# Byte addresses for the experts' weights, and second layers issued one block later

## The chip, the cores and the metric

The kernel runs on one core of a Trainium2 chip. The metric is the device time in microseconds of one execution, as the median of several runs. Engines are named as in the profile: PE is the matrix engine (PEld its weight loads, PEq and PEldq what its instruction queue does besides), DVE the vector engine, ACT the scalar engine, POOL the general one, SP the one that only starts DMAs.

## What is computed

The input (16 sequences of 113 tokens, 256 wide, 1808 tokens in all) goes through eight layers with residuals. Two of them are layers of experts, and only those are touched:

```python
# layer 0: 15 experts, 3 for each token
h = jnp.einsum('td,efd->etf', xt, fc1_w) + fc1_b[:, None, :]        # 256 -> 512
xh, g = (h[..., :F], h[..., F:])
a = jax.nn.gelu(g, approximate=False) * xh * geglu_mult[:, None, :]  # 256
yexp = jnp.einsum('etf,edf->etd', a, fc2_w) + fc2_b[:, None, :]      # 256 -> 256
y = jnp.einsum('etd,te->td', yexp, comb)
# layer 3: 8 experts, 1 for each token
for e in range(n_experts):
    h = jax.nn.relu(xt @ w1[e] + b1[e])                              # 256 -> 1024
    y = h @ w2[e] + b2[e]                                            # 1024 -> 256
    out = out + ((sel_t == e).astype(xt.dtype) * wgt_t)[:, None] * y
```

## The kernel before

Float32 numbers are carried as two float16 halves, a high and a low one, and a product is three matmuls (`mm3`, L455 to L459): high by high, high by low, low by high. In the profile these are lines L457, L458 and L459, for all products of the kernel, so that the tile names tell which product it is. In this text three such matmuls are called a three.

A stage before the experts (`stage_route`) sorts the tokens by expert into blocks of 128 and gives each block its expert's number, in a small table that is known only when the kernel runs. `stage_experts` then goes over the blocks: 57 in the layer of 15 experts (tiles m0x_...), 23 in the layer of 8 (m3x_...). For each block n:

- POOL gathers the 128 token rows from DRAM with an indirect DMA (`gather`, xg, four buffers) and copies the expert's bias (`bias`, b1, two buffers). In its program gather n+3 stands before bias n, and bias n waits until `lo_ready` says that block n-2 is through.
- PE turns the tokens (`turn`, four transposes, L1511, into pt), ACT copies them into SBUF (`take_tokens`, L1562, xb).
- PE does the first layer (`first`, into ph, two buffers): in m0x 4 x 2 threes of 128 columns, in m3x 8 x 2.
- m0x: ACT makes the gate with Gelu (L1573), DVE the product (L1607, a), ACT its high half (L1578, ah), DVE the low half (L1619, al). m3x: ACT makes the high half with Relu straight from ph (L1582, eight instructions), DVE the same in float32 (L1613, eight), then the low half (L1619).
- PE does the second layer (`second`, into py, two buffers): in m0x 2 threes of 256 columns, in m3x 8.
- DVE scales the result (L1625, yo), SP stores it (L1644).

All weights of all experts lie in SBUF, `w1_hi`, `w1_lo`, `w2_hi` and `w2_lo`. Which one a matmul reads depends on the expert's number, so that PE's instruction stream holds register instructions ahead of matmuls, which compute the address. [...]

The order of the work is written out by hand for PE: turn 0, turn 1, first 0, and then for each n: turn n+2, first n+1, second n. ACT and DVE follow: ACT takes tokens n+2 and does `hidden` n+1 (gate and high half); DVE does `hidden` n+1 (product and low half) and then output n. Other layers' weights are prepared between blocks (`prepare`, m0x alone).

Of the kernel before, what the change touches and what calls it, by code (L numbers as in the profile page):

```python
# [6 lines left out]
F16 = mybir.dt.float16  # L7
# [9 lines left out]
D = 256  # L17
# [1102 lines left out]


# [314 lines left out]
def stage_experts(nc, core, m, prepare=None):  # L1436

    N, NF, FH = m.blocks, m.NF, m.FH  # L1440
    with Stage(nc, m.name + "x") as st:
        two, four = range(2), range(4)
# [6 lines left out]
        a_hi, a_lo = ([st.sb(f"{n}{p}", [128, FH, 128], F16) for p in two] for n in ("ah", "al"))  # L1449
# [8 lines left out]
                "y_out", "stored"))  # L1458
        if prepare is not None:
            prepare = prepare(st)  # L1460
        with nc.Block() as block:  # L1461
            @block.gpsimd
            def _(pool):
                if prepare is not None:
                    prepare.on_pool(pool)

                def gather(at):
                    p, before = at.of(4)

# [24 lines left out]
            @block.tensor  # L1494
            def _(pe):
# [9 lines left out]
                def turn(at):  # L1505
                    (p, before), (q, uses) = at.of(2), at.of(4)
                    pe.wait_ge(gathered[q], uses * 16 + 16)

                    need(pe, xb_ready[p], before)
# [5 lines left out]
                def first(at, e):  # L1515
                    p, before = at.of(2)
                    pe.wait_ge(xb_ready[p], before + 1)
# [10 lines left out]
                def second(at, e):  # L1528
                    p, before = at.of(2)

                    need(pe, y_out[p], before)
                    pe.wait_ge(hi_ready[p], before + 1)
                    pe.wait_ge(lo_ready[p], before + 1)
                    for f in range(FH):
                        w = [w[:, bass.ds(e, 1), f, :].rearrange("p a n -> p (a n)") for w in (m.w2_hi, m.w2_lo)]
                        last = mm3(pe, py[p][:, 0:D], a_hi[p][:, f, :], a_lo[p][:, f, :], w[0], w[1],
                                   f == 0, f == FH - 1)
                    last.then_inc(y_ready[p], 1)

                turn(At(0, 0))  # L1540
                turn(At(0, 1))
                ahead = expert(0)
                first(At(0, 0), ahead)
# [12 lines left out]
            def _(act):  # L1556
                def take_tokens(at):
                    (p, before), (q, uses) = at.of(2), at.of(4)
                    act.wait_ge(turned[q], uses + 1)

                    need(act, h_ready[p], before)
# [3 lines left out]
                def hidden(at):  # L1565
                    p, before = at.of(2)
                    act.wait_ge(h_ready[p], before + 1)
                    act.wait_ge(b1_ready[p], before + 1)
                    if m.gelu:

                        need(act, a_ready[p], before)
                        for f in range(FH):
                            ins = act.activation(gate[p][:, f, :], ph[p][:, FH + f, :], ACT.Gelu,  # L1573
                                                 bias=b1[p][:, 0, FH + f:FH + f + 1], scale=1.0 / WS)
                        ins.then_inc(gate_ready[p], 1)
                        act.wait_ge(a_ready[p], before + 1)
                        need(act, y_ready[p], before)
                        act.activation(a_hi[p][:], act32[p][:], ACT.Copy).then_inc(hi_ready[p], 1)  # L1578
                    else:
                        need(act, y_ready[p], before)  # L1580
                        for f in range(FH):
                            ins = act.activation(a_hi[p][:, f, :], ph[p][:, f, :], ACT.Relu,  # L1582
                                                 bias=b1[p][:, 0, f:f + 1])
                        ins.then_inc(hi_ready[p], 1)

                def step(at):
                    take_tokens(at + 2)
                    hidden(at + 1)

                take_tokens(At(0, 0))  # L1590
                take_tokens(At(0, 1))
                hidden(At(0, 0))
                for n in range(N - 2):
                    step(At(0, n))
                    if prepare is not None:
                        prepare.on_scalar(act, n)
                hidden(At(0, N - 1))

            @block.vector
            def _(dve):  # L1600
                def hidden(at):
                    p, before = at.of(2)
                    if m.gelu:
                        dve.wait_ge(gate_ready[p], before + 1)
                        need(dve, hi_ready[p], before)
                        for f in range(FH):
                            ins = dve.scalar_tensor_tensor(act32[p][:, f, :], ph[p][:, f, :], b1[p][:, 0, f:f + 1],  # L1607
                                                           gate[p][:, f, :], ALU.add, ALU.mult)
                        ins.then_inc(a_ready[p], 1)
                    else:  # L1610
                        dve.wait_ge(hi_ready[p], before + 1)
                        for f in range(FH):
                            ins = dve.tensor_scalar(act32[p][:, f, :], ph[p][:, f, :], b1[p][:, 0, f:f + 1], 0.0,  # L1613
                                                    ALU.add, ALU.max)
                        ins.then_inc(a_ready[p], 1)
                        dve.wait_ge(a_ready[p], before + 1)
                    dve.wait_ge(hi_ready[p], before + 1)
                    need(dve, y_ready[p], before)
                    dve.tensor_tensor(a_lo[p][:], act32[p][:], a_hi[p][:], ALU.subtract).then_inc(lo_ready[p], 1)  # L1619

                def output(at):
                    p, before = at.of(2)
                    dve.wait_ge(y_ready[p], before + 1)
                    need(dve, stored[p], before * 16)
# [3 lines left out]
                def step(at):  # L1628
                    hidden(at + 1)
                    output(at)  # L1630

                hidden(At(0, 0))
                for n in range(N - 1):
                    step(At(0, n))
                    if prepare is not None:
                        prepare.on_vector(dve, n)
                output(At(0, N - 1))
# [1356 lines left out]
```

## Time and profile before

| | us |
|---|---|
| three runs | 1645.15, 1646.43, 1638.35 |
| median | 1645.15 |
| the profiled execution | 1638.66 |
| its span in the profile | 1636.9 |
| m0x stage, first weight matmul to last (57 blocks) | 457.5 to 635 |
| m3x stage, the same (23 blocks) | 1448.7 to 1607.2 |
| PE busy over the span | 1145.5 (70%) |
| DVE | 1097.2 (67%) |
| ACT | 676.8 (41%) |
| POOL | 477.6 (29%) |

The span is what the profiler saw between the first and the last instruction; 1.8 us lie around it. Times in the views are microseconds from the span's start. PE's durations overlap, since matmuls are pipelined: what counts is the distance from one start to the next.

### The profile page before, as it was taken

Reading aid. Unit: us, or ns where it says so; the run is one execution under the profiler, and the core shown is the slowest. Engines: PE = TensorE matmul, PEld = TensorE weight load, DVE = VectorE, ACT = ScalarE, POOL = GpSimd, SP = SyncE. Lnnn points to the kernel's source line nnn. Section 1 sums busy time; section 2 is a strip of 40 time slices with the busy share of each in tenths; the row PEclk is TensorE's granted clock in tenths of the full one; section 3 lists DMA queues with packets and bytes.
Section 4 is the critical chain, followed back from the end, with each engine's and each line's share of the span. In section 5 each row is a group of like instructions: output and inputs, shape, how many; then the busy total and the mean of one; then the engine's idle time right before and its main releaser. Section 6 shows DMA issues by size and latency. Waiting matters only on the chain. (4 is left out here: it accounts for less than half of the span.)

```text
span 1636.9 us, 31503 instructions
## 1 busy us (share of the span) xinstructions
PE 1145.5 (70%) x9868; PEld 802.0 (49%) x9868; DVE 1097.2 (67%) x2322; ACT 676.8 (41%) x1332; POOL 477.6 (29%) x614
## 2 busy tenths in 40 slices
PE   4514877773489998776757866466588885479991
PEld 2211232223367775454446744244467774468881
DVE  4864999984836554657867655787677776445552
ACT  4514655552045443214426522343366554124430
POOL 0042777762344443720001100000133322222103
PEclk9557999995589999886977977687565555579996
DMA  6500000001032333311000000000022221111113
GB/s 213 180 2 10 1 1 0 1 1 46 13 130 86 112 87 128 90 33 78 1 1 1 1 0 0 0 0 0 28 85 95 77 78 52 46 30 44 44 28 107
DMA packets 33969, 78.92 MB, mean 48 GB/s; under 512 B 6840, under 2 KB 22900, under 8 KB 30964
## 3 DMA queue, kind: packets, MB, share of 16 engines
q1 hardware_dynamic: 26800, 57.51, 10.2%
q0 software_dynamic: 6912, 18.88, 4.2%
q8 instruction: 69, 1.13, 0.3%
q10 hardware_dynamic: 144, 1.05, 0.2%
q14 instruction: 44, 0.35, 0.1%
HBM read 61.38 MB, written 16.04 MB: 47 GB/s over the span
## 5 line engine op out<-in xcount | busy, mean ns | idle before, releaser
L942 POOL TENSOR_TENSOR scan_ch<-scan_hs,scan_ct 128x452 f32<-128x452 f32 x128 | 143.5, 1142 | 58.6 <-DVE scan_hs L1054 41.7
L967 PE MATMUL scan_py<-scan_ch,ident 128*128 128x452 f32 x256 | 131.5, 604 | 40.7 <-POOL scan_ch L942 31.0
L1054 DVE TENSOR_TENSOR_SCAN scan_hs<-scan_abar,scan_bx 128x452 f32<-128x452 f32 x128 | 132.8, 1077 | 0.7 <-ACT scan_abar L1016 0.5
L2524 POOL TENSOR_TENSOR mha_prob_lo<-mha_prob,mha_prob_hi 113x452 f16<-113x452 f32 x64 | 65.5, 1044 | 137.8 <-ACT mha_prob_hi L2685 137.8
L457 PE MATMUL m0x_ph<-m0x_xb,m_w_hi 128*128 128x128 f16 x456 | 103.5, 228 | 0.2
L458 PE MATMUL m0x_ph<-m0x_xb,m_w_hi 128*128 128x128 f16 x456 | 100.0, 221 | 0.0
L459 PE MATMUL m0x_ph<-m0x_xb,m_w_lo 128*128 128x128 f16 x456 | 99.8, 220 | 0.0
L1613 DVE TENSOR_SCALAR m3x_a<-m3x_ph,m3x_b 128x128 f32<-128x128 f32 x184 | 49.7, 342 | 73.9 <-ACT m3x_ah L1582 73.9
L967 PEld LDWEIGHTS scan_py<-scan_ch,ident 128*128 128x128 f32 x256 | 41.2, 194 | 111.3 <-POOL scan_ch L942 99.9
L1016 ACT ACTIVATE scan_abar<-ssm_dt,ssm_a 128x448 f32<-128x448 f32 x128 | 80.6, 638 | 23.0 <-DVE scan_hs L1054 21.7
L1046 DVE TENSOR_TENSOR scan_bx<-scan_pb,ssm_dx 128x452 f32<-128x452 f32 x128 | 72.8, 609 | 12.2 <-PE scan_pb L954 12.2
L1607 DVE SCALAR_TENSOR_TENSOR m0x_a<-m0x_ph,m0x_b,m0x_gate 128x128 f32<-128x128 f32 x114 | 34.7, 346 | 65.5 <-ACT m0x_gate L1573 65.1
L1582 ACT ACTIVATE m3x_ah<-m3x_ph,m3x_b 128x128 f16<-128x128 f32 x184 | 50.1, 383 | 65.8 <-PE m3x_ph L459 65.8
L457 PE MATMUL m3x_ph<-m3x_xb,m_w_hi 128*128 128x128 f16 x368 | 76.5, 227 | 0.2
L458 PE MATMUL m3x_ph<-m3x_xb,m_w_hi 128*128 128x128 f16 x368 | 74.9, 223 | 0.0
L459 PE MATMUL m3x_ph<-m3x_xb,m_w_lo 128*128 128x128 f16 x368 | 74.9, 222 | 0.0
L2517 POOL MEMSET mha_v_hi<- 113x768 f16 x1 | 0.7, 738 | 244.3 <-POOLq L638 244.3
L1473 POOL DMA_INDIRECT m0x_xg<-m_rows,m0x_idx x57 | 55.6, 975 | 44.6 <-POOL m0x_idx L1471 44.6
L1011 ACT ACTIVATE scan_ct<-scan_pc 128x452 f32<-128x452 f32 x64 | 35.0, 547 | 73.0 <-POOL scan_ch L942 40.7
L1672 POOL DMA_INDIRECT shared_got<-m_out,m_slot x48 | 51.8, 1078 | 27.4 <-issue 23.0
L457 PE MATMUL m3x_py<-m_w_hi,m3x_ah 128*128 x184 | 51.6, 280 | 6.2 <-DVE m3x_al L1619 5.8
L457 PEld LDWEIGHTS m0x_ph<-m0x_xb,m_w_hi 128*128 x456 | 44.0, 97 | 23.9 <-issue 1.5
(699 smaller groups left out, 4022.7 us busy)
## 6 DMA issues: line engine op xcount, KB each, us to landing
mha_wbuf<-m3w SPq DMA_DIRECT2D x16, 1024.0 KB, 4.6
tok_wbuf<-m0w SPq DMA_DIRECT2D x15, 768.0 KB, 4.3
m_out<-m0x_yo SPq DMA_DIRECT2D x57, 128.0 KB
m_out<-m3x_yo SPq DMA_DIRECT2D x23, 128.0 KB, 1.7
m_rows<-m0f_parts SPq DMA_DIRECT2D x4, 448.0 KB
m_rows<-m3f_parts SPq DMA_DIRECT2D x4, 448.0 KB
out<-h SPq DMA_DIRECT2D x4, 448.0 KB
tok_pt_f<-patches SPq DMA_DIRECT2D x1, 1728.0 KB, 8.2
```

Source lines behind the costliest of these rows:

```text
L457: pe.matmul(out, w_hi, x_hi, start=start, stop=False)
L458: pe.matmul(out, w_hi, x_lo, start=False, stop=False)
L459: return pe.matmul(out, w_lo, x_hi, start=False, stop=stop)
L942: pool.tensor_tensor(ch[r][:], hs[r][:], ct[n % 2][:], ALU.mult).then_inc(weighed, 1)
L967: pe.matmul(py[c][:, 0:GT], core.ident[:], ch[u % R][:], start=n == 0, stop=n == NS - 1).then_inc(summed, 1)
L1016: act.activation(abar[c][:, 0:GT].rearrange("p (b t) -> p b t", t=L)[:, :, 1:L], ssm.dt[:, c, cols].rearrange("p (b t) -> p b t", t=L)[:, ...
L1046: dve.tensor_tensor(bx[u % R][:], pb[n % 2][:, 0:GT], ssm.dx[:, c, cols], ALU.mult).then_inc(drive, 1)
L1054: dve.tensor_tensor_scan(hs[u % R][:], abar[c][:, 0:GT], bx[u % R][:], 0.0, ALU.mult, ALU.add).then_inc(scanned, 1)
L1473: pool.indirect_dma_start(xg[p][:], None, m.rows[:, :], bass.IndirectOffsetOnAxis(ap=idx[p][:, 0:1], axis=0)).then_inc(gathered[p], 16)
L1582: ins = act.activation(a_hi[p][:, f, :], ph[p][:, f, :], ACT.Relu, bias=b1[p][:, 0, f:f + 1])
L1672: pool.indirect_dma_start(self.got[j][k][:], None, m.out[:, :], bass.IndirectOffsetOnAxis(ap=m.slot[:, b, k:k + 1], axis=0)).then_inc(self ...
L2524: pool.tensor_tensor(prob_lo[g][:], prob[g % 2][:], prob_hi[g][:], ALU.subtract).then_inc(p_low, 1)
```

## The change

Addresses of experts' weights: the tensor is seen as bytes, the place is given in bytes, and the slice is seen as float16 again.

```diff
+    def first(self, e, k, f):
+        at, n = 2 * (k * self.NF + f) * 128, KC * self.NF * 256
+        return [w[:].rearrange("p e k n -> p (e k n)").bitcast(mybir.dt.uint8)[:, bass.ds(e * n + at, 256)].bitcast(F16)
+                for w in (self.w1_hi, self.w1_lo)]
+
+    def second(self, e, f):
+        at, n = 2 * f * D, self.FH * 2 * D
+        return [w[:].rearrange("p e f n -> p (e f n)").bitcast(mybir.dt.uint8)[:, bass.ds(e * n + at, 2 * D)].bitcast(F16)
+                for w in (self.w2_hi, self.w2_lo)]
...
-                            w = [w[:, bass.ds(e, 1), k, f * 128:(f + 1) * 128].rearrange("p a n -> p (a n)")
-                                 for w in (m.w1_hi, m.w1_lo)]
-                            last = mm3(pe, ph[p][:, f, :], w[0], w[1], xb[p][:, k, :], xb[p][:, KC + k, :],
+                            last = mm3(pe, ph[p][:, f, :], *m.first(e, k, f), xb[p][:, k, :], xb[p][:, KC + k, :],
```

The order on PE. The second layer of block n now follows the first layers of n+1 and n+2; the halves of the activations (ah, al) have three buffers instead of two:

```diff
-        a_hi, a_lo = ([st.sb(f"{n}{p}", [128, FH, 128], F16) for p in two] for n in ("ah", "al"))
+        a_hi, a_lo = ([st.sb(f"{n}{r}", [128, FH, 128], F16) for r in three] for n in ("ah", "al"))
...
+        taken = a_ready if m.gelu else lo_ready
...
-                    wait_alone(pool, core, lo_ready[p], before)
+                    wait_alone(pool, core, taken[p], before)
...
-                    need(pe, lo_ready[p], before)
+                    need(pe, taken[p], n // 2)
...
+                turn(0)
+                turn(1)
+                e[0] = expert(0)
+                first(0, e[0])
+                turn(2)
+                e[1] = expert(1)
+                first(1, e[1])
                 for n in range(N):
-                    e = ahead
-                    if n + 2 < N:
-                        turn(At(0, n + 2))
-                    if n + 1 < N:
-                        ahead = expert(n + 1)
-                        first(At(0, n + 1), ahead)
-                    second(At(0, n), e)
+                    if n + 3 < N:
+                        turn(n + 3)
+                    if n + 2 < N:
+                        e[n + 2] = expert(n + 2)
+                        first(n + 2, e[n + 2])
+                    second(n, e[n])
```

`taken` is what tells that ph may be written again: in m0x the product on DVE (instead of the low half), in m3x still the low half. ACT and DVE follow in their loops over n. ACT, m0x: high half n+1, tokens n+3, gate n+2; m3x: tokens n+3, high half n+2. DVE:

```diff
+                for n in range(-2, N):
+                    if m.gelu and 0 <= n + 1 < N:
+                        low(n + 1)
+                    if n + 2 < N:
+                        product(n + 2)
+                        if not m.gelu:
+                            low(n + 2)
+                    if n >= 0:
+                        output(n)
+                    if prepare is not None and n >= 0:
+                        prepare.on_vector(dve, n)
```

The high and the low half of block n wait, from n = 3 on, for the second layer of n-3, whose buffer they take. What is prepared for other layers comes in the same n as before, on ACT and DVE behind the steps above.

## Rows read from the trace of the kernel before

**Rows 1.** Busy time by stretches: us, each engine's busy us (instructions), clock, DMA share, GB/s.
```profile
463.00:631.30 168.30, 166.59 (x1869) 127.95 (x1867) 91.96 (x246) 86.56 (x224) 75.13 (x156) 1.00 0.31 90
...
1463.50:1596.80 133.30, 132.71 (x1573) 111.71 (x1571) 74.78 (x201) 55.48 (x180) 22.09 (x51) 1.00 0.13 38
```
**Rows 2.** Timeline of weight loads, first layer, m0x: start, us, engine, line, operation; three threes apart.
```profile
540.87 0.10 PEld L457 LDWEIGHTS m0x_ph<-m0x_xb,m_w_hi 128*128 x1
...
541.58 0.10 PEld L457 LDWEIGHTS m0x_ph<-m0x_xb,m_w_hi 128*128 x1
```
**Rows 3.** Timeline of weight loads, start of a first layer in m3x; two threes apart.
```profile
1515.27 0.10 PEld L457 LDWEIGHTS m3x_ph<-m3x_xb,m_w_hi 128*128 x1
...
1515.61 0.10 PEld L457 LDWEIGHTS m3x_ph<-m3x_xb,m_w_hi 128*128 x1
```
**Rows 4.** Lines L457 and L459 in m0x: count, ns min/median/max, first and last start.
```profile
L457 PEldq FUSED_REGOPS  x568: 46/46/51, 457.2 to 631.5; - x190
...
L459 PEldq ALU_OP  x456: 32/32/36, 457.3 to 631.0; - x152
```
**Rows 5.** Lines L457 and L458 in m3x, the same columns.
```profile
L457 PEldq FUSED_REGOPS  x365: 46/46/46, 1449.1 to 1596.4; - x183
...
L458 PEldq ALU_OP  x178: 32/32/32, 1459.7 to 1603.0; - x178
```
**Rows 6.** Timeline of weight loads, from first to second layer, m0x and m3x.
```profile
545.50 0.10 PEld L459 LDWEIGHTS m0x_ph<-m0x_xb,m_w_lo 128*128 x1
545.75 0.10 PEld L457 LDWEIGHTS m0x_py<-m_w_hi,m0x_ah 128*128 128x128 f16 x1 [0.16 <-issue]
545.84 0.10 PEld L458 LDWEIGHTS m0x_py<-m_w_lo,m0x_ah 128*128 128x128 f16 x1
...
1512.23 0.10 PEld L459 LDWEIGHTS m3x_ph<-m3x_xb,m_w_lo 128*128 x1
1512.45 0.10 PEld L457 LDWEIGHTS m3x_py<-m_w_hi,m3x_ah 128*128 128x128 f16 x1
1512.57 0.10 PEld L458 LDWEIGHTS m3x_py<-m_w_lo,m3x_ah 128*128 128x128 f16 x1
```
**Rows 7.** Who waited for whom in m0x, 457 to 632: us in total, times, longest.
```profile
PE m0x_py L457 <- DVE m0x_al L1619: 1.6, 3, 0.9
```
**Rows 8.** Start of m3x: timeline of PE, and the stretch after it.
```profile
1459.65 0.27 PE L457 MATMUL m3x_py<-m_w_hi,m3x_ah 128*128 x1 [2.69 <-DVE m3x_al L1619]
...
1459.50:1463.50 4.00, 3.85 (x21) 2.85 (x22) 3.21 (x9) 0.00 (x0) 1.54 (x4) 0.58 0.11 33
```
**Rows 9.** End of m0x: timeline of PE.
```profile
631.14 0.22 PE L459 MATMUL m0x_ph<-m0x_xb,m_w_lo 128*128 128x128 f16 x1
...
633.82 0.28 PE L457 MATMUL m0x_py<-m_w_hi,m0x_ah 128*128 x1 [1.63 <-DVE m0x_al L1619]
```
**Rows 10.** End of m3x: timeline of PE and DVE, and two stretches.
```profile
1596.62 0.22 PE L459 MATMUL m3x_ph<-m3x_xb,m_w_lo 128*128 128x128 f16 x1
...
1601.28 1.23 DVE L1619 TENSOR_TENSOR m3x_al<-m3x_a,m3x_ah 128x1024 f16<-128x1024 f32 x1
1602.42 0.42 DVE L1625 TENSOR_SCALAR m3x_yo<-m3x_py 128x256 f32<-128x256 f32 x1
...
1602.74 0.27 PE L457 MATMUL m3x_py<-m_w_hi,m3x_ah 128*128 x1 [3.12 <-DVE m3x_al L1619]
...
1596.80:1599.50 2.70, 2.70 (x25) 2.27 (x24) 0.41 (x2) 2.18 (x8) 0.00 (x0) 1.00 0.14 49
...
1602.70:1607.20 4.50, 4.45 (x24) 3.14 (x24) 0.14 (x1) 0.00 (x0) 0.00 (x0) 0.62 0.08 29
```
**Rows 11.** Timeline of POOL in m0x, and the gathers' landing in m3x.
```profile
501.87 0.19 POOL L1482 COPY m0x_b<-m_b 128x4 f32 x1 [0.90 <-DVE m0x_al L1619]
...
504.92 0.19 POOL L1482 COPY m0x_b<-m_b 128x4 f32 x1 [0.93 <-DVE m0x_al L1619]
...
DMA to landing us min/median/max: 2.7/2.9/3.8
```

More of the change, by code:

```diff
@@ L1441, in stage_experts @@
     with Stage(nc, m.name + "x") as st:
-        two, four = range(2), range(4)
+        two, three, four = range(2), range(3), range(4)
         idx = [st.sb(f"idx{p}", [128, 1], U32) for p in four]
@@ L1503, in expert, with turn @@
                                               "the router's stage bounds each number by the last expert")
[L1505 to L1509, printed above, removed]
+                def turn(n):
+                    p, q = n % 2, n % 4
+                    pe.wait_ge(gathered[q], n // 4 * 16 + 16)
+                    need(pe, xb_ready[p], n // 2)
                     for c in range(2 * KC):
@@ L1513, in turn, with first @@
                     last.then_inc(turned[q], 1)
-                def first(at, e):
-                    p, before = at.of(2)
-                    pe.wait_ge(xb_ready[p], before + 1)
-                    need(pe, lo_ready[p], before)
+                def first(n, e):
+                    p = n % 2
+                    pe.wait_ge(xb_ready[p], n // 2 + 1)
+                    need(pe, taken[p], n // 2)
                     for f in range(NF):
                         for k in range(KC):
-                            w = [w[:, bass.ds(e, 1), k, f * 128:(f + 1) * 128].rearrange("p a n -> p (a n)")
-                                 for w in (m.w1_hi, m.w1_lo)]
-                            last = mm3(pe, ph[p][:, f, :], w[0], w[1], xb[p][:, k, :], xb[p][:, KC + k, :],
+                            last = mm3(pe, ph[p][:, f, :], *m.first(e, k, f), xb[p][:, k, :], xb[p][:, KC + k, :],
@@ L1525, in first, with second @@
                                        k == 0, k == KC - 1)
                     last.then_inc(h_ready[p], 1)
[L1528 to L1533, printed above, removed]
+                def second(n, e):
+                    p, r = n % 2, n % 3
+                    need(pe, y_out[p], n // 2)
+                    pe.wait_ge(hi_ready[p], n // 2 + 1)
+                    pe.wait_ge(lo_ready[p], n // 2 + 1)
@@ L1534, in second @@
                     for f in range(FH):
-                        w = [w[:, bass.ds(e, 1), f, :].rearrange("p a n -> p (a n)") for w in (m.w2_hi, m.w2_lo)]
-                        last = mm3(pe, py[p][:, 0:D], a_hi[p][:, f, :], a_lo[p][:, f, :], w[0], w[1],
+                        last = mm3(pe, py[p][:, 0:D], a_hi[r][:, f, :], a_lo[r][:, f, :], *m.second(e, f),
                                    f == 0, f == FH - 1)
                     last.then_inc(y_ready[p], 1)
-                turn(At(0, 0))
@@ L1556, in _, with take_tokens @@
             def _(act):
[L1557 to L1561, printed above, removed]
+                def take_tokens(n):
+                    p = n % 2
+                    act.wait_ge(turned[n % 4], n // 4 + 1)
+                    need(act, h_ready[p], n // 2)
                     act.activation(xb[p][:].rearrange("p c n -> p (c n)"), pt[p][:, 0:2 * KC * 128],
@@ L1563, in take_tokens @@
                                    ACT.Copy).then_inc(xb_ready[p], 1)
[L1565 to L1568, printed above, removed]
-                    if m.gelu:
[L1571 to L1594, printed above, removed]
+                def take_gate(n):
+                    p = n % 2
+                    act.wait_ge(h_ready[p], n // 2 + 1)
+                    act.wait_ge(b1_ready[p], n // 2 + 1)
+                    need(act, a_ready[p], n // 2)
+                    for f in range(FH):
+                        ins = act.activation(gate[p][:, f, :], ph[p][:, FH + f, :], ACT.Gelu,
+                                             bias=b1[p][:, 0, FH + f:FH + f + 1], scale=1.0 / WS)
+                    ins.then_inc(gate_ready[p], 1)
@@ new lines, in high @@
+                def high(n):
+                    p, r = n % 2, n % 3
+                    if n >= 3:
+                        act.wait_ge(y_ready[(n - 3) % 2], (n - 3) // 2 + 1)
+                    if m.gelu:
+                        act.wait_ge(a_ready[p], n // 2 + 1)
+                        act.activation(a_hi[r][:], act32[p][:], ACT.Copy).then_inc(hi_ready[p], 1)
+                        return
+                    act.wait_ge(h_ready[p], n // 2 + 1)
+                    act.wait_ge(b1_ready[p], n // 2 + 1)
+                    for f in range(FH):
+                        ins = act.activation(a_hi[r][:, f, :], ph[p][:, f, :], ACT.Relu, bias=b1[p][:, 0, f:f + 1])
+                    ins.then_inc(hi_ready[p], 1)
@@ new lines, in _ @@
+                take_tokens(0)
+                take_tokens(1)
+                if m.gelu:
+                    take_gate(0)
+                    take_tokens(2)
+                    high(0)
+                    take_gate(1)
+                else:
+                    high(0)
+                    take_tokens(2)
+                    high(1)
+                for n in range(N):
+                    if m.gelu and n + 1 < N:
+                        high(n + 1)
+                    if n + 3 < N:
+                        take_tokens(n + 3)
+                    if n + 2 < N:
+                        take_gate(n + 2) if m.gelu else high(n + 2)
@@ L1595, in _, with product @@
                     if prepare is not None:
                         prepare.on_scalar(act, n)
-                hidden(At(0, N - 1))
             @block.vector
             def _(dve):
-                def hidden(at):
-                    p, before = at.of(2)
+                def product(n):
+                    p = n % 2
                     if m.gelu:
-                        dve.wait_ge(gate_ready[p], before + 1)
-                        need(dve, hi_ready[p], before)
-                        for f in range(FH):
+                        dve.wait_ge(gate_ready[p], n // 2 + 1)
+                    else:
+                        dve.wait_ge(hi_ready[p], n // 2 + 1)
+                    need(dve, hi_ready[p], n // 2)
+                    for f in range(FH):
+                        if m.gelu:
@@ L1607, in hidden @@
                             ins = dve.scalar_tensor_tensor(act32[p][:, f, :], ph[p][:, f, :], b1[p][:, 0, f:f + 1],
                                                            gate[p][:, f, :], ALU.add, ALU.mult)
[L1609 to L1612, printed above, removed]
+                        else:
                             ins = dve.tensor_scalar(act32[p][:, f, :], ph[p][:, f, :], b1[p][:, 0, f:f + 1], 0.0,
@@ L1614, in hidden @@
                                                     ALU.add, ALU.max)
[L1615 to L1624, printed above, removed]
+                    ins.then_inc(a_ready[p], 1)
@@ new lines, in low, with output @@
+                def low(n):
+                    p, r = n % 2, n % 3
+                    dve.wait_ge(a_ready[p], n // 2 + 1)
+                    dve.wait_ge(hi_ready[p], n // 2 + 1)
+                    if n >= 3:
+                        dve.wait_ge(y_ready[(n - 3) % 2], (n - 3) // 2 + 1)
+                    dve.tensor_tensor(a_lo[r][:], act32[p][:], a_hi[r][:], ALU.subtract).then_inc(lo_ready[p], 1)
+                def output(n):
+                    p = n % 2
+                    dve.wait_ge(y_ready[p], n // 2 + 1)
+                    need(dve, stored[p], n // 2 * 16)
@@ L1625, in output @@
                     dve.tensor_scalar(yo[p][:], py[p][:, 0:D], 1.0 / (WS * WS), None,
                                       ALU.mult).then_inc(y_out[p], 1)
[L1628 to L1635, printed above, removed]
+                for n in range(-2, N):
[8 more added lines that the diff above has]
+                    if prepare is not None and n >= 0:
```

5 lines of the change are left out of this document (1 added, 4 removed).

## The prediction

> **What bounds the kernel now.** I read the page's table of slices first, then the busy time by stretches, then the timeline of the two stages that the change touches. The kernel is a row of stages, each ended by a barrier, so what the change is worth is read in the two stages that it touches: the layer of 15 experts (m0x, 57 blocks) and the layer of 8 experts (m3x, 23 blocks). From the start of the weight work of block 0 to the last second layer they take 457.4 to 635 us and 1448.7 to 1607.2 us, together 336 of the 1636.9 us. In both, PE is busy in 99% of the stretch at the full clock, while DVE, ACT and POOL are near half [rows 1]. So the other engines are cover, and PE has to be looked at from inside.
>
> PE busy is not PE at its peak. In m0x the weight loads of the first layer come in threes, and one three follows the other after 0.23 to 0.24 us [rows 2]. The same three matmuls (128 columns, same clock) follow each other after 0.17 us at the start of a first layer in m3x, where PE had a stock of issued instructions [rows 3]. So 0.07 us of each 0.236 are not the array's. What stands between the loads are register instructions: 568 fused ones and, for the first layers alone, 456 single ones in m0x: one fused for each of the 57 x 10 threes, and one single beside it [rows 4]. One fused instruction takes 46 ns, one single instruction 32 ns. The bound in first layers is PE's instruction stream. In the second layers a matmul streams 256 columns and 25 of them go in 2.7 us, 0.108 us each [rows 10]: 0.33 us for a three, more than the addresses need, so there PE gets ahead with its issuing. Waits for other engines are rare: 1.6 us in m0x in three places beside the last block [rows 7], 2.7 us at the start of m3x [rows 8], and one before each stage's last second layer [rows 9, 10].
>
> **The change part by part.**
>
> *Addresses.* [...] In m0x 568 - 2 x 57 = 454 fused ones become single. In m3x 365 fused ones are there, about 16 for each block: the first layer's, since 23 x 24 threes would have 552; the second layer's addresses there already are single ones [rows 5]. 365 - 23 = 342 become single. That is 796 instructions, at 46 - 32 = 14 ns: **11.1 us**. All of it counts in m0x, since the stream is the bound there all the time. In m3x it counts too: 8 x 0.33 + 16 x 0.17 + 0.22 for turning the tokens = 5.6 us of array work stand against about 6.5 us for a block (133.3 us for some 20.5 blocks), so the array would have to gain another 0.9 us before it was the bound, and the addresses give it 0.2.
>
> The price of one address can be bounded by a place where the same step is seen with both kinds. From the last load of a first layer to the loads of the second layer there lie the same waits; in m0x the first address is a fused one, in m3x a single one. The first load comes after 0.25 and 0.22 us, the load after it, with one more single address, after 0.34 us in both [rows 6]. So the single one gives its load 0.03 us earlier, but what follows comes hardly earlier: between 0 and 0.03 us each, 0 to 24 us in all. I take the difference of the durations, which lies between them and is measured for exactly these instructions.
>
> [...]
>
> *The order.* The second layer of block n is issued after the first layer of n+2 instead of n+1, and the tokens of n+3 are turned ahead. The number of matmuls, waits, DMAs and ACT, DVE and POOL instructions for a block stays, and no DMA is added. In the middle of a stage this hides waits that hardly exist, so it is worth little there. It matters at the ends.
> - m0x, start and middle: the waits for the low half of the activations, 1.6 us in three places [rows 7], go. What PE would wait for next, in first(n+2), is only the float32 product of block n, a first layer (2.1 us) older. **1.6 us**.
> - m0x, last block: after its last first-layer matmul (631.14) PE has one second layer to do, six matmuls or 0.65 us, and then waits 1.6 us for the low half [rows 9]. Now it has two. **0.65 us**.
> - m3x, start: PE waits 2.7 us for the low half of block 0, and the clock is then 0.58 over the next 4 us [rows 8]. In this stage first(2), the first layer of block 2, waits for the low half of block 0 too, because ph has two buffers. So the wait stays, with the turning of block 3 done inside it (0.3 us). In the slow stretch PE now does first-layer work, where a three takes 0.33 us (twice 0.17) instead of 0.22, and not second-layer work, where it takes 0.65 instead of 0.33. Over the 3.4 us that it lasts (a mean of 0.58 over 4 us is 3.4 us at half speed) this loses 1.1 us instead of 1.7. Together **1.0 us**.
> - m3x, last block: the last first-layer matmul ends at 1596.84 and the low half at 1602.5, 5.7 us later; PE has one second layer in between, 2.6 us, waits 3.1 us and then runs its last 24 matmuls at a mean clock of 0.62, in 4.5 us [rows 10]. After the change it has two second layers, 5.25 us, to do in these 5.7 us. But DVE does the output of block 20 behind the low half of block 22, and the last second layer needs that output's buffer: DVE would be through with it at +6.0 (as with the output at 1602.42 now), and PE start at +6.1 instead of +5.9. The wait is 0.9 us, and if the clock holds over it, the layer takes 2.6 us. End at +8.7 with one second layer more inside it, against +10.35: 10.35 - 8.7 + 2.6 = **4.2 us**; 2.3 us if the clock still falls.
>
> *What moves beside it.* POOL now starts the bias copy after the product (m0x) instead of after the low half, so earlier; its gathers have time: in m0x POOL does one round for a block, every 3.0 us, and waits 0.9 us for the low half in it [rows 11]; a gather's tokens are turned three blocks after it is issued, now two, so 6 us for a landing of 2.9 (in m3x) [rows 11]. DVE's order puts the low half of n+1 ahead of the product of n+2, ACT's the high half ahead of the tokens and the gate; each has half of its time free [rows 1]. I cost this at nothing. If that cover were gone, each lost 0.1 us for a block would be 8 us. SP's stores wait for the same outputs as before.
>
> The sum: 11.1 + 1.6 + 0.65 + 1.0 + 4.2 = **18.6 us**. The profiled execution took 1638.66 us around a span of 1636.9; it would take 1620. The median of the three runs is 1645.15, and two of the three lie near it; against it the forecast is **1626.5 us**.
>
> **The rivals.**
> - A, the addresses give nothing: what follows an address is paced by something else (the 0.34 us equal in both stages [rows 6] speak for it, the 0.17 us in rows 3 against). Only the ends are left, 7.4 us: 1637.7 us. [...]
> - B, the whole 0.03 us by which the load comes earlier is gained at each address: 796 x 0.03 = 24 us, sum 31 us, 1614 us. For it speaks the 0.25 against 0.22; against it that the load after is not earlier.
> [...]
> - D, the end of m3x keeps its fall of the clock and the start gains nothing: 18.6 - 2.9 = 15.7 us, 1629.5 us. The clock fell after waits of 2.7 us and 3.1 us [rows 8, 10] and of 1.6 us in m0x [rows 9]; a wait of 0.9 us is not in the trace.
>
> **How the numbers follow.** About 0.5%, 8 us, is what a measurement of this kernel can tell from no change. Forecast 0.58, A 0.15, B 0.10, C 0.05, D 0.12. Forecast, B, D and a quarter of A (it lies at the edge, 7.4 us) give 0.84 for faster, the rest of A 0.11 for same, C 0.05 for slower. The range goes from B (1614) to A (1638); the runs of before lie 8 us apart, which is inside it.
>
> **What would show it.** Right: almost no fused instructions with line 457 (about 114 and 23 left of 568 and 365); threes in m0x after 0.22 us; 3.0 us for a block of m0x instead of 3.1; a wait before m3x's last second layer of about 1 us, and its matmuls 0.11 us apart. Wrong: fused instructions as many as before (C), the same 0.236 us with single ones (A), 0.20 us (B), PE waits inside m0x for xb, a or xg, which would mean that the new order has made another engine late.

## The result, and the profile after

The changed kernel takes 1627.07 us in the median (1631.85, 1619.72, 1625.43, 1628.7), the kernel before 1643.84 us (its three runs and one of 1642.53 beside these). The ratio is 0.9893, with a 95% interval of 0.9858 to 0.9929: 1.1% less. The forecast was 1626.5. The profiled execution took 1631.85 us around a span of 1630.1.

Both stages of experts are as full as before, only shorter. Busy time by stretches, after, as in [rows 1] (window, length, busy us of PE, PEld, DVE, ACT and POOL with instructions, clock, DMA share, GB/s):

```profile
464.00:623.90 159.90, 159.06 (x1849) 134.70 (x1846) 89.72 (x245) 86.44 (x224) 77.27 (x155) 1.00 0.32 94
1464.70:1591.10 126.40, 126.31 (x1532) 113.34 (x1529) 74.32 (x200) 54.77 (x179) 22.01 (x51) 1.00 0.13 39
```

The threes of a first layer in m0x, after (weight loads of line L457, one for each three; against [rows 2]): three of them take 0.67 us where they took 0.71.

```profile
540.16 0.10 PEld L457 LDWEIGHTS m0x_ph<-m0x_xb,m_w_hi 128*128 x1
...
540.83 0.10 PEld L457 LDWEIGHTS m0x_ph<-m0x_xb,m_w_hi 128*128 x1
```

The register instructions of line L457 after, first two rows m0x, then two of m3x (count, ns min/median/max, first and last start; against [rows 4, 5]). Of 570 fused ones (FUSED_REGOPS) in the whole of m0x (568 in the window of [rows 4]) 114 are left, of 368 in the whole of m3x 23, and what is left takes 37 ns instead of 46. The rest have become single ones (ALU_OP); their number together is the same as before, 674 and 594:

```profile
L457 PEldq ALU_OP  x560: 32/32/41, 458.0 to 626.7; - x187
L457 PEldq FUSED_REGOPS  x114: 37/37/47, 458.1 to 626.5; - x114
...
L457 PEldq ALU_OP  x571: 32/32/41, 1449.5 to 1599.0; - x191
L457 PEldq FUSED_REGOPS  x23: 37/37/47, 1449.6 to 1587.2; - x23
```

PE's waits in the two stages behind the first gathers, those over 0.3 us, after (engine, tile and line, releaser: us in total, times, longest; against [rows 7 to 10]): the three in the middle of m0x are gone, the one before its last second layer is 1.1 instead of 1.6 us, the one before m3x's is 0.8 instead of 3.1, and the one at the start of m3x has stayed and stands now before a first layer. Behind it the clock is at 0.58 over 4 us, as before (last row: that stretch).

```profile
PE m3x_ph L457 <- DVE m3x_al L1652: 3.0, 1, 3.0
PE m0x_py L457 <- DVE m0x_al L1652: 1.1, 1, 1.1
PE m3x_py L457 <- DVE m3x_yo L1658: 0.8, 1, 0.8
...
1461.30:1465.30 4.00, 3.97 (x41) 3.92 (x42) 2.90 (x8) 0.00 (x0) 1.54 (x5) 0.58 0.11 33
```

The end of m3x, after (timeline of PE and DVE, then a stretch, against [rows 10]). The last first-layer matmul ends at 1591.22, two second layers fill the time to 1596.6, the low half of block 22 is ready at 1596.92, and then PE still waits for the output of block 20, which DVE does behind it. The last layer runs at the full clock, where before it had 0.62.

```profile
1591.00 0.22 PE L459 MATMUL m3x_ph<-m3x_xb,m_w_lo 128*128 128x128 f16 x1
...
1595.70 1.22 DVE L1652 TENSOR_TENSOR m3x_al<-m3x_a,m3x_ah 128x1024 f16<-128x1024 f32 x1
...
1596.84 0.75 DVE L1658 TENSOR_SCALAR m3x_yo<-m3x_py 128x256 f32<-128x256 f32 x2
1597.39 0.27 PE L457 MATMUL m3x_py<-m_w_hi,m3x_ah 128*128 x1 [0.77 <-DVE m3x_yo L1658]
...
1597.30:1600.00 2.70, 2.61 (x24) 2.27 (x24) 0.29 (x1) 0.00 (x0) 0.00 (x0) 1.00 0.28 97
```

**A measure that is finer than the time.** Executions of one kernel on one chip lie up to 22 us apart, so the terms of the sum can't be read from totals. They can from the two stages. As length of a stage I take the start of its first first-layer matmul to the start of its last second-layer matmul, the first number of a row of L457 for `ph` and the last of one of L459 for `py`. Before (first, last start at the end of a row; m0x, then m3x):

```profile
L457 PE MATMUL m0x_ph<-m0x_xb,m_w_hi x456: 219/227/314, 457.5 to 631.0; 128*128 128x128 f16 x152
L459 PE MATMUL m0x_py<-m_w_hi,m0x_al x114: 270/273/421, 462.9 to 634.6; 128*128 x114
...
L457 PE MATMUL m3x_ph<-m3x_xb,m_w_hi x368: 219/227/311, 1448.7 to 1596.5; 128*128 128x128 f16 x184
L459 PE MATMUL m3x_py<-m_w_hi,m3x_al x184: 270/272/421, 1459.9 to 1606.9; 128*128 x184
```

After:

```profile
L457 PE MATMUL m0x_ph<-m0x_xb,m_w_hi x456: 216/216/314, 458.4 to 623.6; 128*128 128x128 f16 x152
L459 PE MATMUL m0x_py<-m_w_hi,m0x_al x114: 270/272/273, 465.3 to 627.1; 128*128 x114
...
L457 PE MATMUL m3x_ph<-m3x_xb,m_w_hi x368: 216/219/314, 1449.9 to 1590.9; 128*128 128x128 f16 x184
L459 PE MATMUL m3x_py<-m_w_hi,m3x_al x184: 270/273/273, 1466.0 to 1599.9; 128*128 x184
```

Read in this way, every profile of this study gives (us; more than one number is more than one profiled execution):

| kernel | m0x | m3x | against before |
|---|---|---|---|
| before | 177.1, 177.1 | 158.2, 158.2 | |
| order alone | 174.7 | 153.9 | -6.7 |
| bytes alone | 171.3, 171.5 | 154.1, 154.4 | -9.7 |
| the change | 168.7, 168.5, 168.4 | 150.0, 149.1, 150.1 | -17.0 |
| three addresses for a three | 227.6 | 194.7 | +87.0 |
| one address for a three | 131.6 | 133.6 | -70.1 |
| the change, ph free early | 168.8, 169.4 | 148.0, 148.7 | -17.9 |
| the same, product by halves | 169.1, 168.5 | 146.1, 146.7 | -20.1 |

The same kernel gives the same stage within 1 us; half of the ten pairs and threes of numbers agree within 0.3, the others differ by 0.6 to 1.0. So a term of 2 us can be read in this way, and one of 0.5 us can't. Much of the spread arises at the start of m3x, where the granted clock is 0.50 over the first 2 us in each of the 14 profiles: in the first profile of the change the granted clock of the first three stretches of 2 us is 0.50, 0.50, 0.70, in the second 0.50, 0.66, 1.00, and that m3x is 0.9 us shorter.

### The profile page after: what moved, and what is told of

Same layout as the page of the kernel before. It is cut to its first block and busy times, and to the rows that moved or that the text cites. A ratio compares the mean times of both kernels' runs of the same rounds, so it can differ in the third digit from the quotient of the medians.

```text
span 1630.1 us, 31525 instructions
## 1 busy us (share of the span) xinstructions
PE 1137.5 (70%) x9868; PEld 814.8 (50%) x9868; DVE 1096.1 (67%) x2322; ACT 676.5 (42%) x1332; POOL 477.9 (29%) x614
## 3 DMA queue, kind: packets, MB, share of 16 engines
q1 hardware_dynamic: 26800, 57.51, 10.3%
## 5 line engine op out<-in xcount | busy, mean ns | idle before, releaser
L457 PE MATMUL m0x_ph<-m0x_xb,m_w_hi 128*128 128x128 f16 x456 | 99.2, 220 | 0.2
L458 PE MATMUL m0x_ph<-m0x_xb,m_w_hi 128*128 128x128 f16 x456 | 99.1, 219 | 0.0
L459 PE MATMUL m0x_ph<-m0x_xb,m_w_lo 128*128 128x128 f16 x456 | 98.7, 218 | 0.0
L457 PE MATMUL m3x_ph<-m3x_xb,m_w_hi 128*128 128x128 f16 x368 | 74.4, 225 | 3.0 <-DVE m3x_al L1652 3.0
L459 PE MATMUL m3x_ph<-m3x_xb,m_w_lo 128*128 128x128 f16 x368 | 74.6, 225 | 0.0
L458 PE MATMUL m3x_ph<-m3x_xb,m_w_hi 128*128 128x128 f16 x368 | 74.5, 225 | 0.0
L1586 ACT ACTIVATE m0x_gate<-m0x_ph,m0x_b 128x128 f32<-128x128 f32 x114 | 35.6, 363 | 36.7 <-PE m0x_ph L459 33.9
L457 PE MATMUL m3x_py<-m_w_hi,m3x_ah 128*128 x184 | 50.1, 272 | 0.8 <-DVE m3x_yo L1658 0.8
```

The lines of the kernel that those rows point to most:

```text
L457: pe.matmul(out, w_hi, x_hi, start=start, stop=False)
L458: pe.matmul(out, w_hi, x_lo, start=False, stop=False)
L459: return pe.matmul(out, w_lo, x_hi, start=False, stop=stop)
```

## The experiments

They ran on three chips, four kernels at a time, each beside the kernel before on the same chip; a ratio is always to that.

**1. The order alone.** The changed kernel with the old way of addressing:

```diff
-last = mm3(pe, ph[p][:, f, :], *m.first(e, k, f), xb[p][:, k, :], ...
+w = [w[:, bass.ds(e, 1), k, f * 128:(f + 1) * 128].rearrange("p a n -> p (a n)")
+     for w in (m.w1_hi, m.w1_lo)]
+last = mm3(pe, ph[p][:, f, :], w[0], w[1], xb[p][:, k, :], ...
```

(and the same in `second`).

> The changed order with the old way of addressing (element numbers, so one fused register instruction and one addition for each three matmuls). My theory: the order is worth its waits at the ends of both stages, 7.4 us, so about 1636.4 us against 1643.8 for the kernel before; the three stays at 236 ns in m0x, the wait before the last second layer of m3x is about 1 us and the clock holds there. Rival (the order gives nothing in the start of m3x, and the fall of the clock remains at its end): about 1640 or more. Rival (addresses give nothing, all of the gain is the order's): the time of the full change, about 1627.

Measured: 1640.04 us, ratio 0.9991 (0.9964 to 1.0018), which can't be told from no change. The stages tell it: 2.4 us less in m0x, 4.3 in m3x, 6.7 together of 7.4. The three stays where it was, as the weight loads of m0x show (L457, two threes in 0.47 us):

```profile
541.53 0.10 PEld L457 LDWEIGHTS m0x_ph<-m0x_xb,m_w_hi 128*128 x1
...
542.00 0.10 PEld L457 LDWEIGHTS m0x_ph<-m0x_xb,m_w_hi 128*128 x1
```

The wait at the end of m3x is 0.7 us, and the clock is 1.00 behind it (PE's waits, then the stretch of the last second layer):

```profile
PE m3x_py L457 <- DVE m3x_yo L1661: 0.7, 1, 0.7
...
1609.70:1612.40 2.70, 2.60 (x24) 2.27 (x24) 0.30 (x1) 0.00 (x0) 0.00 (x0) 1.00 0.28 97
```

So the end belongs to the order, and the rival that gives all of the gain to it is out. The other rival has the right total (1640) for a wrong reason: by it the clock would still fall at the end.

**2. Byte addresses alone**, in the old order, with `m.first` and `m.second` put into the kernel before; run twice, on different chips.

> The old order with byte addresses (two single additions for each three matmuls, 798 fused instructions fewer). My theory, with the 12 ns less for each three that the trace of the change shows: 9 to 11 us less, about 1634 us; the three at 225 ns; the wait of 3.1 us before the last second layer of m3x stays as it was. Rival (addresses give nothing): 1643.8. Rival (a fused instruction costs 30 ns more than an addition): 24 us less, 1620.

> The old order with byte addresses, beside the full change. Its stages were 6.1 and 3.9 us shorter than before, while its first times were only 5.8 us below (interval 0.8 to 10.8). If the time follows the stages it is 10 us under before, ratio 0.994, and 7 us above the full change.

Measured: first 1638.61 us, ratio 0.9965 (0.9934 to 0.9995), then 1622.74 us, ratio 0.9932 (0.9907 to 0.9958). The stages agree with each other better than the times: 5.7 and 4.0 us less, 9.7 together. The old end of m3x is still there (timeline of PE, then the stretch behind it):

```profile
1592.89 0.27 PE L457 MATMUL m3x_py<-m_w_hi,m3x_ah 128*128 x1 [3.11 <-DVE m3x_al L1626]
...
1592.50:1597.00 4.50, 4.07 (x24) 2.85 (x24) 0.49 (x2) 0.00 (x0) 0.00 (x0) 0.69 0.08 29
```

The first time misses the expected 1634, which the stages would give. Parts 1 and 2 together are 16.4 us; the whole change has 17.0. They add up within what the measure can tell: the order gives 6.7 us alone and 7.4 beside bytes alone.

**3. A third address for a three.** The second matmul reads the same weights by an address of its own:

```diff
-last = mm3(pe, ph[p][:, f, :], *m.first(e, k, f), xb[p][:, k, :], xb[p][:, KC + k, :],
-           k == 0, k == KC - 1)
+hi, lo = m.first(e, k, f)
+again = m.w1_hi[:, bass.ds(e, 1), k, f * 128:(f + 1) * 128].rearrange("p a n -> p (a n)")
+pe.matmul(ph[p][:, f, :], hi, xb[p][:, k, :], start=k == 0, stop=False)
+pe.matmul(ph[p][:, f, :], again, xb[p][:, KC + k, :], start=False, stop=False)
+last = pe.matmul(ph[p][:, f, :], lo, xb[p][:, k, :], start=False, stop=k == KC - 1)
```

> The full change with a third address for each three matmuls of the first layers: the second matmul's weights are the same bytes, but their address is worked out once more, by a fused instruction (824 more register instructions). My theory (TensorE's instruction stream is the bound, each register instruction opens a gap of 112 to 124 ns that nothing covers): 92 to 102 us more, about 1724 us, the three at about 340 ns. Rival (the pace is that of the matmuls, register instructions run beside them): no change, 1627, the three at 225 ns.

Measured: 1734.56 us, ratio 1.056 (1.0514 to 1.0605). m0x is 59.1 us longer than with the change, 130 ns for each of 456 added instructions, m3x 45.0 us, 122 ns for each of 368. The rows of line L1539 and the weight loads around them:

```profile
L1539 PEldq FUSED_REGOPS  x456: 46/46/56, 458.8 to 683.0; - x152
...
541.44 0.10 PEld L1538 LDWEIGHTS m0x_ph<-m0x_xb,m_w_hi 128*128 x1
541.59 0.10 PEld L1539 LDWEIGHTS m0x_ph<-m0x_xb,m_w_hi 128*128 x1
541.68 0.10 PEld L1540 LDWEIGHTS m0x_ph<-m0x_xb,m_w_lo 128*128 x1
541.79 0.10 PEld L1538 LDWEIGHTS m0x_ph<-m0x_xb,m_w_hi 128*128 x1
```

An instruction that the profile shows for 46 ns costs more than 120, though the weights that it points to are the same. The stream of register instructions is the bound; the rival by which they run beside the matmuls is out.

**4. One address for a three.** The third matmul takes the high half of the weights, not the low one. The kernel then leaves out the product with the low half, so its result is another one; it serves to time the stream alone:

```diff
-last = mm3(pe, ph[p][:, f, :], *m.first(e, k, f), xb[p][:, k, :], ...
+last = mm3(pe, ph[p][:, f, :], *m.first(e, k, f)[:1] * 2, xb[p][:, k, :], ...
```

> The full change with one address for each three matmuls of the first layers: the third matmul takes the high half of the weights instead of the low half (another result), so 824 additions are gone. My theory (each register instruction takes a slot of some 112 ns of the instruction stream): the pace falls on the three matmuls themselves, 165 ns at the full clock, 60 ns less for each three or 49 us in all, about 1578 us; m0x about 142 us instead of 169, m3x about 128 instead of 150, if vector, scalar engine and the gathers keep up. Rival (the pace is that of weight loads and matmuls, not of register instructions): 1627.

Measured: 1563.4 us, ratio 0.955 (0.9521 to 0.958). m0x is 36.9 us shorter than with the change, m3x 16.1, and now the array is the bound in first layers of both: a three takes 0.167 us from one end of a first layer to the other. The weight loads in m0x, from the second of a layer to the last, 22 steps in 1.23 us, 56 ns each, and the stretch:

```profile
540.56 0.10 PEld L458 LDWEIGHTS m0x_ph<-m0x_xb,m_w_hi 128*128 x1
...
540.68 0.10 PEld L457 LDWEIGHTS m0x_ph<-m0x_xb,m_w_hi 128*128 x1
540.73 0.10 PEld L458 LDWEIGHTS m0x_ph<-m0x_xb,m_w_hi 128*128 x1
540.79 0.10 PEld L459 LDWEIGHTS m0x_ph<-m0x_xb,m_w_hi 128*128 x1
...
541.79 0.10 PEld L459 LDWEIGHTS m0x_ph<-m0x_xb,m_w_hi 128*128 x1
...
463.00:584.00 121.00, 119.71 (x1818) 114.72 (x1816) 87.45 (x241) 81.04 (x222) 73.91 (x154) 1.00 0.44 123
```

The loads of these threes all read one tensor, but that isn't what makes them fast: in the kernel before, threes with both tensors follow each other after 0.17 us too, where PE has instructions in stock [rows 3]: there the first fused instruction starts 0.5 us ahead of its weight load, the sixth 0.1 us, and from the sixth on the lead stays 0.1 us while the step goes to 0.24.

I had expected 60 ns for each three. It was 81 in m0x and 44 in m3x. In m0x the 0.225 us is the usual step, not the mean: here and there a step takes 0.25 to 0.38, and with the second register instruction these steps went as well. The mean step inside a first layer of m0x was 0.236 us with the change and is 0.167 now, 68 ns less; what is missing to 81 lies between the layers. In m3x it was 0.208 us, since about two in five steps had 0.17 us already, where PE comes out of a second layer with instructions in stock [rows 3]. Two waits of PE in m0x are new with this pace, 1.0 us together, for the tokens that ACT copies (xb).

**5. The kernel before, and the change again.** In the first profile of the change the stage behind m0x, the shared experts' (its code is the same), took 111.2 us from its first matmul to that of the next stage, against 101.7 before: it seemed to give back what m0x had won.

> The full change once more, for a second profile. In the first profile the two expert stages became 16.6 us shorter, but the shared experts' stage behind the first of them 9.5 us longer, with matmuls there issued 0.7 us apart for some 20 us though nothing was waited for. If that belongs to the changed kernel (its earlier start of that stage collides with something), the shared stage is again about 9 us longer than before and the span about 1630. If it is an accident of that execution, the shared stage is back at 101.7 us and the span near 1621. Median either way: 1625 to 1629.

> The kernel before, once more, timed and profiled like the others. In its first profile the shared experts' stage took 101.7 us from its first matmul to that of the next stage; in the five profiles of other kernels, which all have the same code there, 109.3 to 115.5. If those belong to the scatter of executions, this profile shows the shared stage anywhere from 101 to 116 us, m0x again at 177.6 and m3x at 158.5 us, and the ratio of the two sets of runs is 1.000 within some 0.3%. If the earlier end of m0x is what lengthens the stage behind it, it is 101 to 103 us again.

> The full change a third time, on one chip with the two kernels that go on from it. The stages m0x and m3x should again take 169.0 and 149.5 to 150.3 us, 16.6 to 17.6 less than before; the ratio to before 0.989 to 0.990 if the rest of the program is not changed by it, 0.991 or more if the shared stage behind m0x takes part of it back.

Measured: the change took 1629.61 us, ratio 0.9914 (0.9885 to 0.9943), and 1617.11 us, ratio 0.9905 (0.9871 to 0.9938); the kernel before against itself 1.0005 (0.9982 to 1.0027). The shared stage:

| chip | kernels profiled | shared stage, us |
|---|---|---|
| a first | order, bytes, the change, three addresses | 115.5, 109.3, 112.3, 113.3 |
| a second | before, one address, ph free early, halves | 100.2, 100.2, 101.2, 100.0 |
| a third | the change, ph free early, halves, bytes | 101.0, 100.0, 100.9, 101.2 |

The second profile of the change had the longer stage again and seemed to say that it belongs to the change; the third chip took that back. The stage is also long for a kernel with the old order and the old end of m0x (bytes alone, 109.3), and for both kernels it is short on another chip. So it doesn't go with the kernel. Whether it goes with the chip or with the hour isn't told, since each chip was used at one time only, and of the first pair of profiles (101.7 and 111.2) the chips aren't known. Nor was the kernel before profiled on the first chip. But its times there speak against a stage that is 10 us shorter than in the others: on that chip the medians gain 14.2 us where the stages gain 17.0 (the change), and 5.2 where they gain 9.7 (bytes alone). So the kernel before seems to have most of the 10 us too, and what the change could give back there is about 3 us; on the third chip it is 15.9 against 17.0 and 10.3 against 9.7, and nothing of it is seen. What the longer stage consists of is seen in the waits of that stretch, first execution of the change:

```profile
ACT shared_gate L1833 <- remote: 25.2, 4, 11.8
...
DVE shared_a L1866 <- remote: 7.4, 2, 6.0
```

Rows with this releaser, for which the profile has no name, stand in the profiles of all five long stages, in this stage alone, and in none of the nine others. What they are was not tried and stays open.

**6. What is left at the ends of m3x.** Two kernels that go on from the change. First, ph counts as free when the product has read it:

```diff
-taken = a_ready if m.gelu else lo_ready
+taken = a_ready
```

Then the product of the first four chunks of features no longer waits for the high half of all eight (DVE then reads chunks 0 to 3 while ACT is at 4 to 7; `half_ready` is a new semaphore):

```diff
 ins = act.activation(a_hi[r][:, f, :], ph[p][:, f, :], ACT.Relu, bias=b1[p][:, 0, f:f + 1])
+if f == FH // 2 - 1:
+    ins.then_inc(half_ready[p], 1)
...
-dve.wait_ge(hi_ready[p], n // 2 + 1)
+dve.wait_ge(half_ready[p], n // 2 + 1)
 for f in range(FH):
+    if not m.gelu and f == FH // 2:
+        dve.wait_ge(hi_ready[p], n // 2 + 1)
```

> The full change, but in m3x the accumulator of the first layers is free once the product has read it, not once the low half is made (the rule that m0x already has). Theory: first(2) starts with the end of product(0) instead of low(0), so the wait at the start of m3x falls from 3.0 to 1.8 us, 1.2 us less for the stage (149.5 to 150.3 become 148.7); in the time 1.2 us, under what these rounds can tell. Rival (bias or transposes are late next): the wait only changes its name and stays 3.0 us.

> free_early again, beside the full change. By its stages (m3x 148.4 us in its first profile, against 149.5 and 150.3) 1 to 2 us less than the full change. Its first times were 26 us below the kernel before, which its stages don't explain (about 18); if that was scatter, the difference to the full change is now 0 to 3 us.

> [...] Theory: at the start of m3x product(0) ends 1.1 us earlier and the wait falls to about 0.7 us; at its end low(22) comes 1.1 us earlier and the wait of 0.8 us before the last second layer is gone; together 3.1 us off m3x against the full change (about 147 us). Rival (the end is held by the output of block 20 or by the next matmul group): the end wait stays 0.5 us or more.

> halves again, beside the full change. By its stages (m3x 146.4 us) 3 to 4 us less than the full change and 2 less than free_early.

Measured: free early 1610.87 us, ratio 0.9843 (0.9814 to 0.9873), then 1615.6 us, 0.9901 (0.9863 to 0.9939); halves 1614.02 us, 0.9864 (0.9834 to 0.9894), then 1614.24 us, 0.9877 (0.9837 to 0.9917). Beside the change on one chip (1617.11) that is 1.5 and 2.9 us, less than these times can tell. The stages can: m3x takes 148.0 and 148.7 us, then 146.1 and 146.7, against a mean of 149.7. With the first edit the wait at the start of m3x is 1.2 us in one profile and 1.7 in the other (expected 1.8). Line and wait of the first:

```profile
1443.03 0.23 PE L457 MATMUL m3x_ph<-m3x_xb,m_w_hi 128*128 128x128 f16 x1 [1.20 <-DVE m3x_a L1641]
```

With both edits DVE starts the product of block 0 in m3x 1.0 us before ACT's last instruction of that block ends, in both profiles, where before it started 0.03 us behind it. One of the two profiles has no wait of PE in m3x but those for gathers, and the other one of 0.6 us at the start (expected 0.7) and none at the end. Once the clock has risen, 3 to 5 us after the stage's first matmul, it doesn't fall again at the start, in either; the stretch that corresponds to the one with 0.58 [rows 8], in the first profile:

```profile
1441.00:1445.00 4.00, 3.92 (x52) 3.35 (x49) 3.68 (x12) 2.96 (x11) 1.70 (x3) 1.00 0.16 33
```

By its stages the kernel with both is the fastest of those with the right result, 3.1 us under the change and 20.1 under the kernel before.

## Why the prediction was right

Its mechanism held, and its terms came out within 2 us. That the total came out within 1 us is in part luck: the sum of 18.6 us was 1.6 too large by the stages (17.0) and 1.8 by the medians (16.8), and it was taken from 1645.15, the median of three runs, which a fourth made 1643.84. The two nearly cancel. By its own steps:

- **The bound** (PE's instruction stream in first layers): right, shown from both sides. One register instruction more for a three cost 87 + 17 = 104 us, one less gave 70.1 - 17.0 = 53.
- **The addresses**, 11.1 us for 796 instructions at 14 ns: measured 9.7 us, the term that was furthest off. In m0x 5.7 us for 454 of them, 12.6 ns each; in m3x 4.0 for 342, 11.6 ns. No run shows which operations make up an address, and so none shows why 2 x 57 and 23 fused ones should stay; what the runs show is their number, and the counts were right (114 and 23 left, to the piece). The sum left out that the 137 fused ones that stay get shorter too, 9 ns each or 1.2 us, which makes the price for each still a little smaller. It also counted the second layers' addresses of m0x, though it said that PE gets ahead there. The gain isn't seen there: the mean step from three to three inside m0x's first layers fell from 0.251 to 0.236 us, which over 399 steps is 6 us, all of that stage's gain.
- **The price of an address.** The difference of the two durations, 14 ns, was near to what was measured, though neither duration is itself a price. With 0.236 us for fused and single [rows 2] and 0.225 for two singles, a single one takes a slot of some 112 ns and a fused one 124, while the profile shows them for 32 and 46; this is an estimate that gives the whole step to the two instructions, and the 122 to 130 ns of kernel 3 agree with it. So do their starts in the first layers of m0x, before: 124 ns in the median from a fused one of line L457 to the single one of L459, 113 from there to the next fused one. Most of a slot, 78 to 80 ns behind the shown duration, is the same for both kinds and falls out of a difference. No run here tells what fills it.
- **m0x, start, middle and last block**, 1.6 + 0.65 = 2.25 us: measured 2.4 (order alone against before), and 2.9 (the change against bytes alone). The waits in the middle were 1.6 us in one execution of the kernel before and 1.3 in the other.
- **m3x, end**, 4.2 us: from the start of the last first-layer matmul to that of the last second-layer one it was 10.0 and 10.3 us before and is 8.9 now with one second layer of 2.6 more inside, which makes 3.7 to 4.0. The step was right in its parts: the output of block 20 behind the low half, a wait of 0.9 (0.8), and a clock that holds over it.
- **m3x, start**, 1.0 us: not told from 1.0 by these runs. What order alone has in m3x, less its end, is 4.3 less 3.7 to 4.0, so 0.3 to 0.6 us; the same subtraction between bytes alone and the change gives 0.7, 0.7 and 1.6 for the three profiles of the change. That the wait stays was right, and so was that the clock falls behind it all the same (0.58 over 4 us, as before). What the sum didn't have is a short loss behind the wait: second(0) started 0.23 us after the end of the low half in all four executions of the old order, first(2) starts 0.43 to 0.44 us after it in order alone and the three of the change. Why was not tried.
- **What moves beside it**, 0: right. With the change the middle of both stages has no new wait, and parts and whole add up.

The rivals: A (the addresses give nothing) would have left bytes alone at no gain; it has 9.7 us in its stages and both its intervals below 1. Nor is the pace that of weight loads and matmuls: with one address left for a three, pairs of them follow each other after 56 ns through whole first layers, at the full clock, against 75 ns with the change, whose three takes 0.225 us. B (30 ns each) is out by the 0.225 us. C (as many fused instructions as before, and a slower kernel) is out by the counts, 114 and 23 left of 570 and 368, and by the time; the change from a fused one to a single one gave 12 ns, while a whole instruction more costs 122 to 130. D (the clock still falls at the end of m3x) is out at the end; its other half, a start that gains nothing, isn't told from the forecast of 1.0 us by these runs. One of its supports was weaker than it seemed: the clock fell behind the wait of 1.6 us at the end of m0x [rows 9] in one execution of the old order and had 1.00 behind the same wait, to the end of the layer, in the three others.

In the time as a whole 17.0 us of stages stand against 14.2 to 16.8 us of medians on the chips; a systematic loss elsewhere isn't seen.

## What to carry to other kernels

Where a matrix engine seems full but small matmuls follow each other more slowly than the same ones do elsewhere in the trace, count the register instructions between them: here each one took a slot of over 110 ns (an estimate from three steps of 0.236, 0.225 and 0.35 us), twice the 56 ns of a weight load and matmul of 128 columns, while its own row shows 32 to 46 ns. A single one in place of a fused one gave about a tenth of the slot, 12 of 124 ns; leaving one out of a three took the usual step in m0x from 0.225 to 0.167 us, which is the array's own pace. And where executions scatter by more than the effect, measure the stage from first to last matmul and not the total: terms of 2 us could be read in this way under a scatter of 20, and terms of half a us could not.

## What had not been expected of the hardware

- The price of one more register instruction on PE, 122 to 130 ns at a shown duration of 46 ns, and what one less gives, 44 and 81 ns, until the array is the bound.
- A stage of unchanged code that takes 100 to 101 us on two chips and 109 to 115 on another, each seen at one time only.
- The clock behind idle stretches of PE. In m3x it was 1.00 over the work behind idle stretches of 0.6 to 1.2 us. It had a mean of 0.72 in the 4 us from the end of one of 1.7 us (the second profile of ph free early, whose first had 1.2 us at the same place and 1.00), and of 0.58 from the end of one of 3.0 us. The fall can come late: behind 3.1 us at the end of m3x the second profile of the kernel before has 1.00 in the first us and 0.63 over 4 us. So the end of m0x, where only 0.9 us of work follows, says less: it has 1.00 there behind 1.1 us, and behind 1.6 us 1.00 in three executions and 0.63 in a fourth.
